# Finer row tables, later shared products, and the last two experts in halves, in a wavelet-attention and mixture-of-experts kernel

## The reference, cut to what matters

```
h = x.reshape(-1, 128)                               # 2048 tokens
scores = sigmoid(h @ gate_w.T)                       # 16 experts
topk_score, topk_ids = top_k(scores.T, 256)          # each expert picks 256 tokens
xin = h[topk_ids]
up = einsum('ecd,efd->ecf', xin, up_w) + up_b        # f = 512
g = einsum('ecd,efd->ecf', xin, gw) + gb
eo = einsum('ecf,edf->ecd', silu(g) * up, down_w) + down_b
out = zeros_like(h).at[topk_ids].add(eo * topk_score)
shared = (silu(x @ sh_gate_w.T) * (x @ sh_up_w.T)) @ sh_down_w.T
return out + shared
```

## Time and profile before

| | |
|---|---|
| median of three runs | 206.62 us (205.88 to 206.64) |
| the profiled execution's own time | 206.66 us |
| its span, first to last instruction | 204.9 us |
| PE busy | 181.7 us (89%) |
| DVE busy | 126.0 us (61%) |
| ACT busy | 92.0 us (45%) |
| POOL busy | 125.5 us (61%) |
| mean granted clock of PE | 0.966 |

### The profile page before, as it was taken

How to read it: one execution, slowest core, us unless ns; L and a number is a source line. 1 busy time by engine, 2 the same in 40 slices (tenths; PEclk the granted TensorE clock), 3 DMA queues, 4 the chain that set the end, 5 groups by cost and what they waited for, 6 DMA issues and landing times.

```text
span 204.9 us, 3617 instructions
## 1 busy us (share of the span) xinstructions
PE 181.7 (89%) x1196; PEld 156.7 (76%) x1196; DVE 126.0 (61%) x430; ACT 92.0 (45%) x240; POOL 125.5 (61%) x191
## 2 busy tenths in 40 slices
PE   6989889999979999998999999999999997948800
PEld 6957679998936577857889999999999996936700
DVE  3989999999777787784667654445444543421300
ACT  2476613468697767210344334444444454331210
POOL 7592006455126475937776888878887777775560
PEclk9999999999999999999999999999999999995875
DMA  5699999700030361114214223233232233332211
GB/s 168 214 408 420 421 419 417 321 4 3 0 117 0 109 214 51 53 31 144 75 44 57 27 42 53 46 40 42 42 58 33 36 40 43 40 40 26 26 13 13
DMA packets 11649, 22.26 MB, mean 109 GB/s; under 512 B 1504, under 2 KB 8800, under 8 KB 11504
## 3 DMA queue, kind: packets, MB, share of 16 engines
q1 hardware_dynamic: 5968, 17.52, 22.4%
q0 software_dynamic: 5664, 4.53, 16.0%
HBM read 17.72 MB, written 4.33 MB: 108 GB/s over the span
## 4 chain that ended last, share of the span: by engine, by line
PE 46%; POOL 13%; DVE 10%; issue 10%; DMA 10%; ACT 6%; POOLq 1%; SPq 0%; ACTq 0%; DVEq 0%
POOL out_dram L543 9%; PE bank L1160 7%; PE bank L1439 7%; PE bank L1440 6%; DMA out_dram<-area,rows 5%; PE bank L1420 5%; PE bank L1115 4%; POOL hT L532 4%; PE bank L1301 4%; PE bank L1313 3%; DMA hT<-h_rows,rows 3%; DMA x_tok<-in_x_dram 2%; PE bank L1263 1%; DVE junk L955 1%; DVE area L812 1%
## 5 line engine op out<-in xcount | busy, mean ns | idle before, releaser
L543 POOL DMA_INDIRECT out_dram<-area,rows x32 | 50.6, 1581 | 17.5 <-issue 6.8
L1091 DVE SCALAR_TENSOR_TENSOR area<-bank,consts,sgate 128x256 f32<-128x256 f32 x64 | 30.9, 483 | 43.4 <-ACT sgate L736 43.3
L736 ACT ACTIVATE sgate<-bank,consts 128x256 f32<-128x256 f32 x64 | 30.3, 474 | 56.4 <-PE bank L1440 56.2
L1439 PE MATMUL bank<-area,wT 128*128 128x256 f32 x128 | 40.2, 397 | 1.2 <-DVE area L1069 0.6
L1420 PEld LDWEIGHTS bank<-wT,area 128*128 128x128 f32 x256 | 38.1, 191 | 3.9 <-DVE area L1091 0.8
L532 POOL DMA_INDIRECT hT<-h_rows,rows x32 | 31.7, 990 | 12.7 <-issue 9.1
L1440 PE MATMUL bank<-area,wT 128*128 128x256 f32 x128 | 39.3, 390 | 0.0
L1420 PE MATMUL bank<-wT,area 128*128 128x128 f32 x256 | 38.6, 275 | 0.4 <-DVE area L1091 0.4
L1440 PEld LDWEIGHTS bank<-area,wT 128*128 128x128 f32 x128 | 25.2, 197 | 3.7
L519 POOL TENSOR_TENSOR sh_hid<-sh_up,sgate 128x64 f32<-128x64 f32 x48 | 13.6, 322 | 15.0 <-ACT sh_up L688 12.4
L1439 PEld LDWEIGHTS bank<-area,wT 128*128 128x128 f32 x128 | 20.5, 198 | 2.7 <-issue 2.2
(11 more groups left out here) (196 smaller groups left out, 259.9 us busy)
## 6 DMA issues: line engine op xcount, KB each, us to landing
wT<-in_weights_dram SPq DMA_DIRECT2D x16, 768.0 KB, 16.4
h_rows<-hrow SPq DMA_DIRECT2D x2, 576.0 KB, 3.6
x_tok<-in_x_dram SPq DMA_DIRECT2D x4, 256.0 KB, 3.9
x_tok<-in_down_b_dram SPq DMA_DIRECT2D x1, 1024.0 KB, 6.1
out_dram<-x SPq DMA_DIRECT2D x4, 256.0 KB, 2.1
hT<-h_rows,rows POOLq DMA_INDIRECT x32, 2.6
out_dram<-area,rows POOLq DMA_INDIRECT x32
sh_wT<-in_shared_dram SPq DMA_DIRECT2D x1, 384.0 KB, 3.2
```

What stands on the lines that cost most here:

```text
L543: pool.indirect_dma_start(out=out_rows, in_=eo[:, e % 2, c, :], in_offset=None, out_offset=bass.IndirectOffsetOnAxis(ap=rows[:, c, e:e + 1 ...
L736: act.activation(sgate_e[:, q % SGB, :], up_bank(q)[:, CAP:2 * CAP], ACT.Silu, bias=biasT[:, 1, j, e:e + 1]).then_inc(s_sil, 1)
L1091: dve.scalar_tensor_tensor(hidden[:, e % 2, j, :], up_bank(q)[:, 0:CAP], biasT[:, 0, j, e:e + 1], sgate_e[:, q % SGB, :], ALU.add, ALU.mul ...
L1439: pe.matmul(up_bank(q)[:, 0:CAP], wT[:, e, 0, j, :], xselT[:, e % 2, :], start=True, stop=True)
```

## The change

1. `GROUPS` becomes four groups of 2, 2, 4 and 8 experts. The three small ones are made ahead of the experts, the one of 8 during them, as before (`LATE`).
2. The last group's `shared_down` moves from ahead of expert 0 to between its steps 1 and 2, with `spread(2)` behind it. DVE's `add_shared` and the third group's `lay_table` and `slot_rows` move into the steps 1 and 2 of expert 0. The fillers ahead of the experts fall from 5 and 3 to 2 and 0.
3. Experts 14 and 15 become four blocks of 128 tokens (`BLOCKS`). Each block has its own transpose, its own four steps on matmuls of 128 columns, its own `add_bias` and `weigh`. A block starts after the last `down` of the block before, and ahead of the transposes of the last three stand eight fillers (`WARM_B`).
4. `eo` has four buffers (`EOB`), and `BETWEEN` gives one gather after expert 6 and one after expert 13, where it gave two and none.

```diff
-    BETWEEN = (2, 2, 2, 2, 2, 2, 2, 1, 1, 1, 1, 1, 1, 0, 0, 0)
+    BETWEEN = (2, 2, 2, 2, 2, 2, 1, 1, 1, 1, 1, 1, 1, 1, 0, 0)
+    EOB = 4
+    HALVED = E - 2
...
-        GROUPS = ((0, 4), (4, 4), (8, 8))
+        GROUPS = ((0, 2), (2, 2), (4, 4), (8, 8))
+        LATE = len(GROUPS) - 1
...
-        eo = carve(2 * CH * C).rearrange("p (s c d) -> p s c d", s=2, c=CH)
+        eo = carve(EOB * CH * C).rearrange("p (s c d) -> p s c d", s=EOB, c=CH)
...
-        FINAL = (E - 1) * FT
+        WHOLE = tuple(range(CH))
+        BLOCKS = [(e, WHOLE) for e in range(HALVED)] + [(e, (c,)) for e in range(HALVED, E) for c in range(CH)]
+        WARM_B = {HALVED + 1: 8, HALVED + 2: 8, HALVED + 3: 8}
...
+            def add_bias(b):
+                e, chunks = BLOCKS[b]
+                c0, n = chunks[0], len(chunks)
+                dve.wait_ge(s_dn, b + 1)
+                if e == 2:
+                    dve.wait_ge(s_hot, 2 * LATE + 4)
+                if e >= EOB:
+                    dve.wait_ge(s_scat, 16 * CH * (e - EOB + 1))
...
+                if b >= HALVED and j == 0:
+                    add_bias(b - 1)
+                    keep_x(b)
                 dve.wait_ge(s_sil, q + 1)
...
-            WARM_I, WARM_E, WARM_S, WARM_L, WARM_C = 5, 3, 6, 3, 4
+            WARM_I, WARM_S, WARM_L, WARM_C = 2, 6, 3, 4
...
-            for q in range(E * FT):
-                e, j = divmod(q, FT)
-                if q == FINAL:
+            for q in range(len(BLOCKS) * FT):
+                b, j = divmod(q, FT)
+                e, chunks = BLOCKS[b]
+                n = len(chunks) * P
+                if b >= HALVED and j == 0:
                     down(q - LAG)
                     down(q - 1)
-                    turn_x(E - 1)
+                    stay_warm(WARM_B.get(b, 0), up_bank(q))
+                    turn_x(b)
...
+                if q == 2:
+                    for t in range(4):
+                        shared_down(LAST, t)
+                    spread(2)
...
-                pe.matmul(up_bank(q)[:, 0:CAP], wT[:, e, 0, j, :], xselT[:, e % 2, :], start=True, stop=True)
+                pe.matmul(up_bank(q)[:, 0:n], wT[:, e, 0, j, :], xselT[:, b % 2, 0:n], start=True, stop=True)
```

More of the change, by code:

```diff
@@ L284, in wavelet_attention_moe @@
         s_gath = [sem(f"s_gath{i}") for i in range(GBUF)]
+        s_gath2 = {e: sem(f"s_gath2_{e}") for e in range(HALVED, E)}
         s_xsT = sem("s_xsT")
@@ L1060, in _ @@
[L1060 removed]
+            hot_his(1)
+            link(hot_lo(2, 0, NT))
             lay_table(1)
+            times_token(2, 0, NT)
             slot_rows(1)
[L1063 to L1069 removed]
+            late_hid(0)
@@ new lines, in _ @@
+            dve.wait_ge(s_db_in, 16)
+            for q in range(len(BLOCKS) * FT):
+                b, j = divmod(q, FT)
+                e, chunks = BLOCKS[b]
+                n = len(chunks) * P
+                if q == 1:
+                    add_shared(LAST - 1, bank[4])
+                if q == 2:
+                    lay_table(2)
+                    slot_rows(2)
+                    add_shared(LAST, bank[6])
+                if b >= HALVED and j == 0:
+                    add_bias(b - 1)
+                    keep_x(b)
+                dve.wait_ge(s_sil, q + 1)
+                if b >= 2:
+                    dve.wait_ge(s_dn, b - 1)
+                dve.scalar_tensor_tensor(hidden[:, b % 2, j, 0:n], up_bank(q)[:, 0:n], biasT[:, 0, j, e:e + 1],
+                                         sgate_e[:, q % SGB, 0:n], ALU.add, ALU.mult).then_inc(s_hid, 1)
+                if q == FT or j == 1 and 1 < b < HALVED:
+                    add_bias(b - 1)
@@ L1444, in _ @@
                     down(q - 1)
-                elif q >= LAG and q not in (FT + 1, FINAL, FINAL + 1):
+                elif q >= LAG and q != FT + 1 and not (b >= HALVED and j < LAG):
                     down(q - LAG)
                 if q == 13:
-                    table(2)
+                    table(LATE)
                 if q == 16:
-                    spread(2)
-                if j == 2 and e + 1 < E - 1:
-                    turn_x(e + 1)
-            for q in range(E * FT - LAG, E * FT):
+                    spread(LATE)
+                if j == 2 and b + 1 < HALVED:
+                    turn_x(b + 1)
+            for q in range(len(BLOCKS) * FT - LAG, len(BLOCKS) * FT):
                 down(q)
```

169 lines of the change are left out of this document (85 added, 84 removed).

## The result

The changed kernel takes 210.13 us (median of 4 runs, 210.12 to 210.39). The kernel before took 206.25 us beside it (4 runs, 205.11 to 206.64). The ratio on record is 1.0214, with an interval of 1.0172 to 1.0257: slower; on 206.66 us that is 4.4 us. From profile to profile it is 206.66 to 210.13, 3.5 us more where 2.3 were forecast.

The account below looks back on a forecast made before the run. PE has no gap up to expert 13, POOL is nearly as full, then late gathers hold PE. Last scatter: 173.15 + 3.7 + 18.0 + 5.2 = 200.05 against 197.75, so 206.66 + 2.3 = 208.9 us; range 205.2 to 210.6.

Parts of the forecast that it names:

- PE is 0.4 us late, not early: Head: expert 0 starts 2.35 us earlier, but moved shared products and DVE waits put expert 1 at 101.8, not 101.38.
- POOL: Scatter pace: expert 1 at 112.8, periods of 6.42 then 5.46, one shorter by 0.96, expert 15 at 194.0.
- A new stall of 0.35 us: Ahead of expert 13: its second gather, issued later, lands at 167.7, and PE waits 0.35 us at the transposes.
- The base, 206.66: The profiled execution of the kernel before, 0.04 over the median, to which the shift of the last scatter was added.
- Sum 6.0 us for each half, where a whole expert took 5.45: Experts 14 and 15: each 128-token half with its fillers takes PE 6.0 us; three periods make 18.0.
- the 207 us that its figures led to: Whole kernel: with the skill page's costs for 128 columns, a half would take 5.5 us and the whole about 207.
- The fillers are not under a wait: Last halves: the last gather lands at 189.5, PE asks behind fillers at 194.1, without them at about 189.7.
- POOL's rival: End: fillers cost nothing, periods fall to 4.5 us, POOL starts the last scatter at 195.9: 204.8 us; chance 0.12.
- The even rival: Halves: ACT and DVE take half the time for half the columns, period 5.45, 206.9 us; chance 0.19.
- The clock's rival: Halves: PE's clock falls in idle stretches; one slow half costs 3.5 us (212.4), all up to 12 (220); chance 0.07.
- I give it nothing: Four `eo` buffers: they remove DVE's wait for scatters, priced at nothing because hidden; without that cover up to 1 us.

Follow-up runs that it names:

- e4: The changed kernel with the old head (three table groups, old order of work up to expert 1): 209.68 us, ratio 1.0184.
- e7: The kernel before with only the new head and four output buffers (experts 14 and 15 whole, old `BETWEEN`, no fillers): 207.28 us, ratio 1.0074.
- e3: The changed kernel with the old `BETWEEN`: 208.81 us, ratio 1.0116.
- e5: The changed kernel with twelve of PE's 18 starting dummy matmuls replaced by six wide ones, to shift its instruction loads: 211.56 us, ratio 1.027.
- e10: The changed kernel with 40 already satisfied semaphore waits ahead of POOL's first gather, to shift its instruction loads: 210.91 us, ratio 1.0258.
- e1: The changed kernel without the eight fillers ahead of each of three halves: 205.61 us, ratio 0.9988.
- e8: The kernel before with only the halves and four output buffers (old head, old `BETWEEN`, no fillers): 206.08 us, ratio 0.9998.
- e2: The changed kernel with experts 14 and 15 whole and no fillers, the rest of the change kept: 219.2 us, ratio 1.0585.
- e11: e8 with two output buffers instead of four: 207.44 us, ratio 1.0083.
- e9: e8 with 14 gathers ahead of the first scatter instead of 12, and five pairs between scatters instead of seven: 210.71 us, ratio 1.0221.
- e12: The kernel before with 14 gathers ahead instead of 12 and six pairs behind, no halves or new head, two output buffers: 210.33 us, ratio 1.0221.

## Why the prediction was right in direction and wrong in size

Its steps, one by one. **"PE is 0.4 us late, not early"**: shown, with 0.67 us at expert 1. Predicted and measured were 94.15 and 94.28 for expert 0, 98.65 and 98.68 for `spread(2)`, 101.8 and 102.05 for expert 1; by the medians, e4 puts the price of the head at 0.45 us and e7 at 207.28 - 206.63 = 0.65, against the kernel before beside it. e7's ratio, 1.0033 to 1.0114, stands for 0.7 to 2.4 us, so the size is known roughly.

**POOL**: predicted 112.8 for expert 1's scatter, 161.3 for expert 9's, 183.1 for expert 13's; measured 113.07, 161.62 and 183.47, so a step of 0.3 that comes from the head.

**"A new stall of 0.35 us"**: this is the step that failed, in its size: the wait was rightly placed, but it was 1.19. The gather was issued 0.3 late, at 165.36 instead of 165.05, which is the delay of POOL's pace; and it landed after 3.5 us, where I had priced every gather by the one of the earlier trace rows at 2.69 and left no room for a late one. PE's transposes came at 168.92 instead of 167.7, and these 1.2 us are what the forecast lacks from profile to profile. e3, where this gather is issued a place earlier, gives 1.3 us back. Why the landing was late is open for this gather; that a load of instructions made it so is the likeliest reading (e5, e10).

**The base, 206.66.** The sum was added to one execution of the kernel before, in which the clock fell at expert 15. By the ratio on record the change is 4.4 us and not 3.5; these 0.9 lie in the kernel before, whose time varies (205.11 to 206.64), and in no step of the sum.

**"Sum 6.0 us for each half, where a whole expert took 5.45"**: 6.12, so 0.4 in three periods. The 128-column operations took 0.37 on ACT (priced 0.39), 0.35, 0.29 and 0.29 on DVE (0.34, 0.28, 0.28). The Trainium skill, "VectorE: DVE Perf Modes" (the TRN2 errata), gives 0.25 and 0.26 us for 128 columns from PSUM; the measured ones lie above it by 0.03 to 0.12, and the 207 us that its figures led to was not what came. The last half took 4.84 from first matmul to scatter (196.38 to 201.22), not 5.2, which takes the 0.4 back.

**"The fillers are not under a wait"**: shown by e1, which gives back 4.5 us. On this the choice between the forecast and POOL's rival hung. That rival was right about where the end then lies: last scatter at 195.9 by its working, 196.54 in e1 and 196.65 in e8. The even rival fell with the 6.12. The clock's rival fell too: 1.00 in the halves with the fillers, and also without them (e1), with idle stretches of up to 0.65 us there. What the Trainium skill says of waits that send the clock back each time ("TensorE: Matmul & The Clock Gate", HAM oscillation) shows in e2, where waits of 4.3 and 4.97 us come with 0.53 and 0.62, and not in the halves.

**The four buffers, "I give it nothing"**: e11 puts them at 1.1 to 1.4 us in the halves without fillers; with the fillers they were not taken out.

So: halves without fillers would have been even, the fillers cost 4.5 us against a fall of the clock that doesn't come, the new `BETWEEN` 1.3 while the fillers are there, the head about 0.5. The halves take away the two waits of the earlier trace rows, but POOL's chain ends only 1.1 us before the old last scatter. None of these versions beats the kernel before. One combination has no run: the old head and the new `BETWEEN` with halves and without fillers.

## What to carry to other kernels

Before a stall is taken away, look at what is next to end: here a chain of scatters, each expert's waiting for the landing of the one before, ends only 1.1 us before the old end, and no order of TensorE's work at the end could win more than that as long as the chain stays as it is. Dummy matmuls that hold a clock up are only worth their place where a trace without them shows it fall. And a transfer that is moved forward on an in-order queue must find the table that it reads: in e9 and e12 POOL stood 3.7 us before one gather that had moved ahead of its table, with all later scatters behind it.

## What the runs showed of the hardware that was not expected

Gathers of one kind, 128 rows each, do not all land alike: 2.5 to 2.9 us as a rule, 3.2 to 4.1 where a load of instructions of 0.02 MB began 1.2 to 2.1 us after the start (18 of 18 in the sixteen traces, behind 102 us). In most places nobody waits for it; ahead of expert 13 a late landing went with a wait of 1.19 us, where an estimate gives 0.3 (1.19 less the 0.9 by which 3.5 exceeds 2.6). The Trainium skill, "Runtime: NRT & Kernel Launch" (Instruction fetch mechanics), has instructions fetched in blocks of 16 KiB over a DMA queue of their own, mostly hidden. The packets of 0.02 MB agree with the block; that such a fetch goes with a late gather, the page does not say. Three gathers onto which e5 and e10 brought a load became 1.2 us slower, which speaks for it as the cause; the load ahead of expert 13 could not be moved away, so there it stays unproven.
